# A graph-attention kernel: the first weight chunk's low part on GpSimd, the scores of unit 0 around two tiles' transposes, h ahead of v's copies

## What is computed

```python
h = jnp.maximum(_layernorm(x, axis=-1), 0.0)
q = h @ Wq.T + bq
k = h @ Wk.T + bk
v = h @ Wv.T + bv
a = q @ k.T * scale + adj + adj          # scale = 1 / sqrt(256)
out = x + jax.nn.softmax(a, axis=-1) @ v
```

## Time and profile before

| | us |
|---|---|
| median of 3 runs (805.50 to 805.56) | 805.5 |
| the profiled execution | 805.57 |
| its span, first to last instruction | 803.7 |

### The profile page before, as it was taken

The page is one execution under the profiler, slowest core; times in us unless marked ns, Lnnn a source line. Parts: engine busy times, 40 slices in busy tenths (PEclk is TensorE's granted clock), DMA queues, the critical chain, the costliest instruction groups (busy, mean ns, idle before and its releaser), DMA issues.

```text
span 803.7 us, 16607 instructions
## 1 busy us (share of the span) xinstructions
PE 798.9 (99%) x6642; PEld 797.1 (99%) x6642; DVE 560.1 (70%) x950; ACT 355.9 (44%) x636; POOL 412.4 (51%) x369
## 2 busy tenths in 40 slices
PE   9999999999999999999999999999999999999998
PEld 8999999999999999999999999999999999999998
DVE  7869666667666766767666766767676676676664
ACT  5764444434443443434344344434444434443375
POOL 4556638091652908256190734719174380926573
PEclk9999999999999999999999999999999999999999
DMA  8522433333332434334243433323333342333300
GB/s 264 193 77 73 118 81 125 93 112 105 100 106 80 135 94 113 93 99 114 85 125 93 121 93 99 110 92 112 97 109 105 88 128 86 110 104 97 90 27 14
DMA packets 46399, 83.57 MB, mean 104 GB/s; under 512 B 5617, under 2 KB 8305, under 8 KB 46321
## 3 DMA queue, kind: packets, MB, share of 16 engines
q1 hardware_dynamic: 45744, 81.71, 34.1%
q10 hardware_dynamic: 576, 0.79, 0.3%
HBM read 78.25 MB, written 4.23 MB: 103 GB/s over the span
## 4 chain that ended last, share of the span: by engine, by line
PE 98%; DVE 1%; ACT 0%; issue 0%; POOL 0%; DVEq 0%; ACTq 0%; POOLq 0%
PE ps L424 51%; PE ps L535 15%; PE ps L536 15%; PE ps L537 15%; PE ps L416 1%; PE ps L402 1%; PE ps L431 0%; ACT x_pair L613 0%; DVE x_res L813 0%; DVE qhl L740 0%; DVE x_res L802 0%; ACT qhl L622 0%; POOL rstd L327 0%; DVE p_lo L793 0%; ACT G L641 0%
## 5 line engine op out<-in xcount | busy, mean ns | idle before, releaser
L424 PE MATMUL ps<-qhl,hT 128*128 128x256 f32 x3072 | 407.8, 283 | 0.6 <-DVE qhl L740 0.6
L424 PEld LDWEIGHTS ps<-qhl,hT 128*128 128x128 f32 x3072 | 383.7, 190 | 0.8 <-DVE qhl L740 0.8
L535 PE MATMUL ps<-v,p_hi 128*128 128x258 f32 x1024 | 290.6, 284 | 0.3 <-DVE p_lo L793 0.3
L536 PE MATMUL ps<-v,p_lo 128*128 128x258 f32 x1024 | 288.9, 282 | 0.0
L537 PE MATMUL ps<-v,p_hi 128*128 128x256 f32 x1024 | 288.2, 281 | 0.0
L680 ACT CAST p_hi<-ps 128x512 fp32r<-128x512 f32 x256 | 150.5, 588 | 261.5 <-PE ps L537 259.8
L392 POOL TENSOR_TENSOR ring_a<-ring_a,m_row 128x512 f32<-128x512 f32 x179 | 226.7, 1310 | 16.1 <-ACT m_row L686 15.4
L748 DVE TENSOR_TENSOR ring_a<-ps,ring_a 128x512 f32<-128x512 f32 x179 | 123.5, 691 | 117.5 <-PE ps L424 116.4
L535 PEld LDWEIGHTS ps<-v,p_hi 128*128 128x128 f32 x1024 | 194.5, 190 | 0.9 <-DVE p_lo L793 0.7
L536 PEld LDWEIGHTS ps<-v,p_lo 128*128 128x128 f32 x1024 | 194.7, 190 | 0.0
L537 PEld LDWEIGHTS ps<-v,p_hi 128*128 128x128 f32 x1024 | 193.4, 189 | 0.0
(11 more groups left out here) (83 smaller groups left out, 334.3 us busy)
## 6 DMA issues: line engine op xcount, KB each, us to landing
ring_a<-in_adj SPq DMA_DIRECT2D x179, 256.0 KB, 2.7
ring_b<-in_adj SPq DMA_DIRECT2D x77, 256.0 KB, 2.7
x_res<-in_x SPq DMA_DIRECT2D x16, 256.0 KB, 3.0
out<-x_res SPq DMA_DIRECT2D x15, 256.0 KB, 2.0
x_pair<-in_x SPq DMA_DIRECT2D x5, 512.0 KB, 4.2
term_row<-term_spill SPq DMA_DIRECT2D x14, 128.0 KB, 3.2
x_third<-in_x SPq DMA_DIRECT2D x2, 512.0 KB, 5.0
w_all<-in_w ACTq DMA_DIRECT2D x2, 257.0 KB, 4.0
```

What stands on the lines that cost most here:

```text
L424: last = nc.tensor.matmul(dst, lhs(a, ib), rhs(c, ib), start=(n == 0), stop=(n == 3 * DB - 1))
L535: nc.tensor.matmul(ps[:, at, 0:VW], hi, v[:, n, 0:VW], start=(n == 0), stop=False)
L536: nc.tensor.matmul(ps[:, at, 0:VW], lo, v[:, n, 0:VW], start=False, stop=False)
```

## The change

It does five things.
1. The low part of weight chunk 0 is made by GpSimd, ahead of `make_rstd(0)`; VectorE makes that of chunk 1 alone. On VectorE `normalize(0)` comes behind the statistics of tiles 2 and 3. The semaphore `s_nlo` becomes two, one for each chunk.
2. `multiply_bias_pair` moves from the middle of `project_first_q` to ahead of `transpose_h(0)`; the biases are kept in `S_BANK`, and the second half of q in the bank next to it.
3. The scores of unit 0 are made by a new `first_scores`: it comes right behind `project_v(0, 0)`, makes the four matmuls of key tile 0 that need no low part of q, then `transpose_h(1)`, then the other eight. Part 1 is transposed into a bank of its own (bank 6), so that its transposes no longer wait for `h_lo(0)` and `transpose_h(2)` no longer for `h_lo(1)`; `project_v(0, 1)`, which writes banks 6 and 7, waits for `h_lo(1)`.
4. On ScalarE `q_hi(0)` and the term bias come ahead of `normalize(1)`, and `normalize(2)` ahead of `h_hi(1)`.
5. On ScalarE `h_hi(2)` comes ahead of `v_hi(0, 0)`.

GpSimd's order is otherwise as before.

```diff
--- before.py
+++ after.py
@@ -129,11 +129,17 @@
         def v_bank(g, pair):
             return V_BANKS[0 if g == GROUPS - 1 else pair]
 
+        def ht_banks(p, at):
+            if p == 1:
+                halves = ps[:, V_BANKS[1], :].rearrange("p (b n) -> p b n", b=DB)
+                return halves[:, :, at.start - GT // 2 * P:at.stop - GT // 2 * P]
+            return ps[:, HT_BANK:HT_BANK + DB, at]
+
         def o_bank(b):
             return S_BANK if b == BLOCKS - 1 else O_BANK
 
         def q_at(b, ob):
-            return ps[:, S_BANK, 0:QB] if (b, ob) == (0, 1) else ps[:, X_BANK, ob * QB:(ob + 1) * QB]
+            return ps[:, S_BANK + 1, 0:QB] if (b, ob) == (0, 1) else ps[:, X_BANK, ob * QB:(ob + 1) * QB]
 
         def early_terms(b):
             return QS * b < GT * EARLY_GROUPS
@@ -162,7 +168,7 @@
         s_ident = sem("ident_made")
         s_const = sem("constants_made")
         s_nhi = sem("wq_wk_hi_written")
-        s_nlo = sem("wq_wk_lo_written")
+        s_nlo = [sem(f"wq_wk_chunk_lo_written{o}") for o in range(DB)]
         s_whi = sem("wv_hi_written")
         s_wlo = sem("wv_lo_written")
         s_bb = sem("bias_products_ready")
@@ -343,6 +349,9 @@
                 nc.gpsimd.tensor_tensor(v[:, t:t + 2, VW:VW + D], v_full[:, pair], v[:, t:t + 2, 0:D].bitcast(f32),
                                         ALU.subtract).then_inc(s_vlo, 1)
 
+            pool.wait_ge(s_nhi, 1)
+            nc.gpsimd.tensor_tensor(wqk[:, 1, 0], wqk_nat[:, 0], wqk[:, 0, 0].bitcast(f32), ALU.subtract)\
+                .then_inc(s_nlo[0], 1)
             make_rstd(0)
             pool.wait_ge(s_bc, 16)
             for ob in range(DB):
@@ -410,10 +419,11 @@
                     pe.wait_ge(s_norm2, max(p, 1))
                 if p > 0:
                     pe.wait_ge(s_norm, p)
-                    pe.wait_ge(s_hlo, p)
+                if p > 1:
+                    pe.wait_ge(s_hlo, 1 if p == 2 else p)
                 for ib in range(DB):
                     for j in tiles:
-                        last = nc.tensor.transpose(ps[:, HT_BANK + ib, j * P:(j + 1) * P],
+                        last = nc.tensor.transpose(ht_banks(p, slice(j * P, (j + 1) * P))[:, ib],
                                                    rows(g)[:, j, ib * P:(ib + 1) * P], ident[:, :])
                     last.then_inc(s_ht, 1)
 
@@ -439,7 +449,7 @@
                 pe.wait_ge(s_nhi, 2)
                 product(1, 0, 0)
                 for ob in range(DB):
-                    pe.wait_ge(s_nlo, ob + 1)
+                    pe.wait_ge(s_nlo[ob], 1)
                     product(ob, 0, 1)
                     last = product(ob, 1, 0)
                 last.then_inc(s_g, 1)
@@ -448,13 +458,13 @@
                 pe.wait_ge(s_bc, 16)
                 for m in range(DB):
                     for ob in range(DB):
-                        last = nc.tensor.matmul(ps[:, S_BANK + 1, m:m + 1], wqk_nat[:, ob, D + m * P:D + (m + 1) * P],
+                        last = nc.tensor.matmul(ps[:, S_BANK, m:m + 1], wqk_nat[:, ob, D + m * P:D + (m + 1) * P],
                                                 bias_cols[:, ob:ob + 1], start=(ob == 0), stop=(ob == DB - 1))
                 last.then_inc(s_bmm, 1)
 
             def multiply_bias_pair():
                 pe.wait_ge(s_bsum, 1)
-                nc.tensor.matmul(ps[:, V_BANKS[1], 0:1], ones[:, :], bias_sum[:, :], start=True, stop=True)\
+                nc.tensor.matmul(ps[:, S_BANK, DB:DB + 1], ones[:, :], bias_sum[:, :], start=True, stop=True)\
                     .then_inc(s_bqk, 1)
 
             def project_q(b):
@@ -468,8 +478,6 @@
 
             def project_first_q():
                 for a, c in ((0, 0), (1, 0), (0, 1)):
-                    if c == 1:
-                        multiply_bias_pair()
                     pe.wait_ge((s_hhi, s_glo, s_hlo)[a + 2 * c], 1)
                     for ob in range(DB):
                         for ib in range(DB):
@@ -498,6 +506,19 @@
                     last = split_product(ps[:, S_BANK + s % 2, k * QB:(k + 1) * QB],
                                          lambda a, ib: hT[:, a, ib, at:at + P],
                                          lambda c, ib: qhl[:, b % 2, c, ib, :])
+                last.then_inc(s_score, 1)
+
+            def first_scores():
+                pe.wait_ge(s_term, 1)
+                pe.wait_ge(s_qhi, DB)
+                for k in range(KT):
+                    for n, (a, c) in enumerate(((0, 0), (1, 0), (0, 1))):
+                        if (k, c) == (0, 1):
+                            transpose_h(1)
+                            pe.wait_ge(s_qlo, 1)
+                        for ib in range(DB):
+                            last = nc.tensor.matmul(ps[:, S_BANK, k * QB:(k + 1) * QB], hT[:, a, ib, k * P:(k + 1) * P],
+                                                    qhl[:, 0, c, ib, :], start=(n + ib == 0), stop=(c == 1 and ib == DB - 1))
                 last.then_inc(s_score, 1)
 
             def turn_max(b):
@@ -542,16 +563,16 @@
 
             multiply_weights()
             pe.wait_ge(s_ident, 1)
+            multiply_bias_pair()
             transpose_h(0)
             multiply_query_bias()
             project_first_q()
             pe.wait_ge(s_wlo, 1)
             pe.wait_ge(s_ulo, 1)
             project_v(0, 0)
-            transpose_h(1)
-            scores(0)
+            first_scores()
             transpose_h(2)
-            pe.wait_ge(s_term, 1)
+            pe.wait_ge(s_hlo, 2)
             project_v(0, 1)
             scores(1)
             for g in range(1, GROUPS):
@@ -601,7 +622,7 @@
                 g, tiles = part_of(p)
                 act.wait_ge(s_ht, DB * p + DB)
                 nc.scalar.activation(hT[:, 0, :, (g * GT + tiles[0]) * P:(g * GT + tiles[-1] + 1) * P],
-                                     ps[:, HT_BANK:HT_BANK + DB, tiles[0] * P:(tiles[-1] + 1) * P],
+                                     ht_banks(p, slice(tiles[0] * P, (tiles[-1] + 1) * P)),
                                      ACT.Relu).then_inc(s_hhi, 1)
 
             def normalize(p):
@@ -642,19 +663,19 @@
             h_hi(0)
             act.wait_ge(s_glo, 1)
             nc.scalar.copy(wv_T[:, 0, :, D:VW], ps[:, V_BANKS[0]:V_BANKS[0] + DB, D:VW]).then_inc(s_uhi, 1)
+            act.wait_ge(s_bqk, 1)
             act.wait_ge(s_bmm, 1)
-            nc.scalar.mul(query_bias[:, :], ps[:, S_BANK + 1, 0:DB], QSCALE).then_inc(s_qb, 1)
+            nc.scalar.mul(query_bias[:, :], ps[:, S_BANK, 0:DB], QSCALE).then_inc(s_qb, 1)
             act.wait_ge(s_qb, 1)
+            nc.scalar.mul(term_bias[:, :], ps[:, S_BANK, DB:DB + 1], QSCALE).then_inc(s_term, 1)
+            q_hi(0)
             normalize(1)
-            q_hi(0)
-            act.wait_ge(s_bqk, 1)
-            nc.scalar.mul(term_bias[:, :], ps[:, V_BANKS[1], 0:1], QSCALE).then_inc(s_term, 1)
+            normalize(2)
             h_hi(1)
-            normalize(2)
+            h_hi(2)
             act.wait_ge(s_wlo, 1)
             act.wait_ge(s_term, 1)
             v_hi(0, 0)
-            h_hi(2)
             v_hi(0, 1)
             normalize(3)
             for g in range(1, GROUPS):
@@ -731,7 +752,7 @@
                 g, tiles = part_of(p)
                 dve.wait_ge(s_hhi, p + 1)
                 hi, lo = (hT[:, a, :, (g * GT + tiles[0]) * P:(g * GT + tiles[-1] + 1) * P] for a in range(2))
-                nc.vector.scalar_tensor_tensor(lo, ps[:, HT_BANK:HT_BANK + DB, tiles[0] * P:(tiles[-1] + 1) * P], 0.0,
+                nc.vector.scalar_tensor_tensor(lo, ht_banks(p, slice(tiles[0] * P, (tiles[-1] + 1) * P)), 0.0,
                                                hi.bitcast(f32), ALU.max, ALU.subtract).then_inc(s_hlo, 1)
 
             def q_lo(b):
@@ -816,13 +837,12 @@
             for j in range(GT // 2):
                 tile_stats(0, j)
             part_stats(0)
-            for ob in range(DB):
-                dve.wait_ge(s_nhi, ob + 1)
-                nc.vector.tensor_tensor(wqk[:, 1, ob], wqk_nat[:, ob], wqk[:, 0, ob].bitcast(f32),
-                                        ALU.subtract).then_inc(s_nlo, 1)
-            normalize(0)
+            dve.wait_ge(s_nhi, DB)
+            nc.vector.tensor_tensor(wqk[:, 1, 1], wqk_nat[:, 1], wqk[:, 0, 1].bitcast(f32), ALU.subtract)\
+                .then_inc(s_nlo[1], 1)
             for j in range(GT // 2, GT):
                 tile_stats(0, j)
+            normalize(0)
             dve.wait_ge(s_ghi, 1)
             nc.vector.scalar_tensor_tensor(G[:, 1], ps[:, V_BANKS[0]:V_BANKS[0] + DB, 0:D], QSCALE,
                                            G[:, 0].bitcast(f32), ALU.mult, ALU.subtract).then_inc(s_glo, 1)
```

## The result

The changed kernel took 807.05 us (median of 20 executions), the kernel before 805.56 (20 executions): 1.49 us more, a ratio of 1.0018 with a 95% interval of 1.0012 to 1.0025. The forecast was 806.9, in a range of 806.0 to 807.7.

The account below looks back on a forecast made before the run. TensorE's own stream, busy 99%, was taken as the bound. T(2) at 14.8 plus a chain of 7.26 put T(3) at 22.06 instead of 20.68; 805.5 and 1.38 is 806.9 us, range 806.0 to 807.7.

Parts of the forecast that it names:

- The hold: On GpSimd, v_lo(0, 0) waits for v_hi(0, 0) and keeps the rstd of part 3 queued; TensorE idles 1.6 us.
- T(2): TensorE's transposes of part 2 (group 1): start at 14.8 instead of 15.47, 0.67 us gained, between 0.4 and 0.85.
- T(3): TensorE's transposes of part 3 (group 2): start at 22.06 instead of 20.68, 1.38 us later.
- T(0): TensorE's transposes of part 0 (tiles 0 and 1): start at 8.42 instead of 8.10; bounds of the shift 0.2 to 0.5.
- the meeting: VectorE add with two SBUF operands meeting a GpSimd instruction: ends 0.55 us behind GpSimd's end, chunk 1 at 6.92.
- The bias pair: TensorE's bias matmuls, moved out of q: wait for bias_sum, done by 8.2, no cost; 0.22 us saved in q.
- 0.3 us would be left as gain: TensorE's v of group 1 begins near 18.9 instead of 19.24, a 0.3 us gain if nothing else moved.
- Rival 1: More waits on GpSimd, ScalarE and VectorE, such as a late T(4): 0.5 us more each, 807.3 to 808; chance 0.10.
- T(4): TensorE's transposes after T(3): wanted at 28.7, normalize(4) ready at 27.3, so no further wait.
- Rival 2: TensorE's clock at 1.2 GHz after the idle stretch: two groups of matmuls cost 2.9 us, 809.8; chance 0.03.
- Rival 3: Rstd of part 3 not held, v_hi(0, 0) done sooner: 0.3 to 0.7 us gained, 804.9 to 805.2; chance 0.06.
- rival 4: Smaller loss if starts are closer than in the rows: 0.3 to 1.0 us, 805.8 to 806.5; chance 0.09.

Follow-up runs that it names:

- e1: Changed kernel with GpSimd's rstd, minus_mean and offset of part 3 moved ahead of v_lo(0, 0); 805.70 us against 805.48 for the kernel before.
- e9: e5 with the first tile's statistics of group 2 moved ahead of h_lo(1) on VectorE; 805.24 us against 805.58 for the kernel before.
- e6: Changed kernel with v_lo(0, 0) made a second time ahead of the rstd of part 3; median 809.06 us against 805.48 for the kernel before.
- e8: Changed kernel with v_lo(0, 0) made a second and third time ahead of the rstd of part 3; 811.06 us against 805.57 for the kernel before.
- e5: Changed kernel with the edits of e1 and e4 together; 805.29 us against 805.57 for the kernel before.
- e4: Changed kernel with VectorE making both weight low parts and normalize(0) ahead of the statistics of tiles 2 and 3 again; 806.71 us against 805.57 before.
- e3: Kernel before with only h_hi(2) moved ahead of v_hi(0, 0) on ScalarE; 807.64 us against 805.48 for the kernel before.
- e7: Kernel before with only chunk 0's low part on GpSimd and normalize(0) behind the statistics; 805.75 us against 805.57 for the kernel before.
- e2: Changed kernel with v_hi(0, 0) back ahead of h_hi(2) on ScalarE; 805.65 us against 805.48 for the kernel before.

## Why the prediction was right, and which terms were off

- **The hold** was the right mechanism in the right place. The chain from T(2) to T(3) was put at 7.26 and is 7.19 (14.70 to 21.89). Its terms: to h_hi(2) 1.07 (put at 1.10), h_hi(2) 0.92 (0.93), v's copies 1.24 (1.22), done at 17.93 for "17 to 18", GpSimd 0.07 behind, v_lo 1.15 up to the rstd (1.19), rstd to the end of offset 1.51 (1.46), ScalarE 0.03 behind and 1.09, TensorE 0.11 behind (0.14).
- **T(0)** was mis-sized: put at 0.32 later, with 0.5 as the upper bound, and 0.52 later in fact. Counted from the cast, GpSimd's low part ends 0.17 later than I had it: it starts 0.16 behind its releaser for 0.08, and takes 1.28 for 1.19. The low part of chunk 1, which on VectorE stands behind the held `var_eps` (below), ends 0.62 behind it for 0.55. The rstd ends 0.60 behind that, about as forecast, though not as I had it (a start at 6.8 and a free run of 0.70): it starts while the low part of chunk 1 still runs, and takes 1.12. T(0) then follows `normalize(0)` by 0.09 instead of 0.15. And I had the meeting touch only adds with two operands in SBUF; VectorE's two-column `var_eps` was held too. GpSimd's timeline of the changed kernel, and VectorE's behind it:

```profile
4.96 1.28 POOL L353 TENSOR_TENSOR wqk<-w_all,wqk 128x514 fp32r<-128x514 f32 x1 [2.87 <-ACT wqk L619]
6.34 1.12 POOL L333 TENSOR_TENSOR rstd<-var_eps,minus_half 128x2 f32<-128x2 f32 x1
```

```profile
5.49 0.77 DVE L740 TENSOR_SCALAR var_eps<-mean_var 128x2 f32<-128x2 f32 x1
6.18 0.68 DVE L841 TENSOR_TENSOR wqk<-w_all,wqk 128x514 fp32r<-128x514 f32 x1
```

- **The held `var_eps`** took 0.77, against 0.17 at 17.52, and ended at 6.26, just behind GpSimd's 6.24. The other runs make this more than one reading: in all six kernels with the low part of chunk 0 on GpSimd this instruction takes 0.59 to 0.77 and ends 0.02 to 0.03 behind GpSimd's, and in the five with it on VectorE it takes 0.17. In e1, where it starts nearer to GpSimd's end, it is the shorter for it:

```profile
5.16 1.28 POOL L353 TENSOR_TENSOR wqk<-w_all,wqk 128x514 fp32r<-128x514 f32 x1 [3.07 <-ACT wqk L617]
5.87 0.59 DVE L738 TENSOR_SCALAR var_eps<-mean_var 128x2 f32<-128x2 f32 x1
```

  The page "SBUF — State Buffer" of the Trainium skill (Who interferes with whom) counts `tensor_scalar` among the instructions that can take the pair of ports for which VectorE and GpSimd stand in each other's way; here it was the one held, and the trace agrees.
- **The bias pair** was put down as done ahead of T(0) at no cost. It was nearly so: bias_sum set its start (the wait of 0.4), and T(0) followed 0.09 behind the end of normalize(0) (8.24).
- **T(2)** was put at 0.67 earlier and is 0.47 earlier. The difference is T(0)'s 0.20; from T(0) to T(2) pass 6.38, as forecast (T(1) waits 0.16, put at 0.2). One step had the wrong engine: T(2) was to wait for VectorE's tiles of `normalize(2)` (end 14.50 in the profile), and ScalarE's tile, which the prediction left out, ends last (14.55).
- **Net**: 7.19 less 5.21 is 1.98 for the hold, less 0.47, is 1.51; measured 1.49, forecast 1.38 (2.05 less 0.67). The forecast is short by the 0.20 of the T(0) term, less 0.07 by which its chain was too long.
- **"0.3 us would be left as gain"** was wrong: e1 shows 0.1 lost in T(3). T(0)'s 0.20 is half of it. The other half is a step that the prediction left out: with h_hi(1) behind normalize(2) on ScalarE, VectorE waits 0.57 us for it ahead of h_lo(1), and the statistics of part 3 stand behind. The variance of part 3 comes 0.7 us later than before (13.49 against 12.78 behind the cast), and T(3) comes 1.64 behind v(2) instead of 1.44. In the changed kernel the hold covered this; e9 moves one of the statistics into that wait and has T(3) 1.44 behind v(2) again. VectorE's timeline of e1:

```profile
15.25 0.69 DVE L753 SCALAR_TENSOR_TENSOR hT<-ps,hT 128x512 fp32r<-128x512 f32 x1 [0.57 <-ACT hT L622]
...
17.70 0.17 DVE L738 TENSOR_SCALAR var_eps<-mean_var 128x4 f32<-128x4 f32 x1
```

- **Rival 1** (more waits behind T(3)) did not come: T(4) starts 6.64 us behind T(3), 6.63 before. **Rival 2** (the clock) did not come for 1.3 us of idleness, in none of 20 executions, but e6 and e8 show that it stood close by; it was put at 2.9 us and costs 1.2 to 2.2 there. The page "TensorE: Matmul & The Clock Gate" of the Trainium skill (What's actually happening) has idleness lower the clock; e6 agrees (granted clock 0.50 behind 2.58 us of idleness). **Rival 3** fell, as each term of the chain was there, and so did **rival 4** (a loss of 0.3 to 1.0), as their sum was 0.07 short of the forecast's.

## What to carry to other kernels

When a step is moved behind another on one engine, look at what queues behind its consumer on the next engine: the moved copies cost nothing where they stood, but GpSimd's low part waited for them with three tiny instructions behind it that TensorE needed. An in-order queue that waits for something late should have nothing urgent behind it; a move of two lines on either engine took all but 0.1 us of T(3)'s delay away. And a gain ahead of a chain of fixed length is a gain only if the chain starts from it: of the 0.85 us by which e5 brings T(2) forward, 0.2 reach T(3).

## What was not expected of the hardware

- Behind the same idle stretch of TensorE the clock fell in some executions of a kernel and not in others. By the length that the profile shows ahead of T(3): 1.3 us, in none of 31 executions (the changed kernel and e4); 1.9 us (e3), in one of six (808.99 against 807.44 to 807.68, clock 0.998); 2.6 us (e6), in two of four; 3.8 us (e8), in four of four. Only e6 and e8 have a profile of such an execution; in the others a mean clock of 0.998 or less, with the longer time, stands for it. It cost 1.2 to 2.2 us each time (e3 and e6 against their other executions, e8 against 805.57, 1.49 and 2.51 together, 809.57).
- Two of e7's eleven executions also had a clock of 0.998 and took 807.73 and 807.26, where its profile shows no idle stretch of TensorE over 0.71 us behind the first microsecond. No profile was taken of these two; what lowered the clock in them stays open.
- A GpSimd subtract that reads SBUF held even a VectorE instruction of two columns until its end: 0.77 instead of 0.17 us, and shorter where it started later, in six kernels.
- The profile's clock column reads 1.00 from the first microsecond on, but TensorE's pace there does not bear it out. The same two `ones` matmuls took 0.63 us in the profile of e1 and 0.38 in that of e2:

```profile
5.65 0.63 PE L409 MATMUL ps<-ones 128*128 128x128 f32 x2
```

```profile
5.64 0.38 PE L411 MATMUL ps<-ones 128*128 128x128 f32 x2
```

  T(0) starts 4.13 us behind the cast in both, so the steps of the table do not hang on it. But a full clock in the earlier trace rows can be taken as shown for the stream behind T(0) only.
